# The last layer's slot numbers read by one load, and four result buffers instead of two

## The chip, the cores and the metric

The kernel runs on one core of a Trainium2 chip. The metric is the device time of one execution in microseconds, the median of several runs. The engines are TensorE (PE, matrix products; PEld is its weight load), VectorE (DVE), ScalarE (ACT), GpSimd (POOL) and SyncE (SP), which issues DMAs. Each runs its own instructions in their order, and they wait for each other through semaphores.

## The reference

Four residual layers in a row on `x` of 64 batches x 64 rows x 256, conditioned by 8 numbers per batch. The change touches the last one only, where each batch goes through one of eight experts:

```python
expert = jnp.argmax(opcode_onehot, axis=-1)
up = jnp.einsum('bsd,bhd->bsh', x, W_up[expert]) + b_up[expert][:, None, :]
gate = jnp.einsum('bsd,bhd->bsh', x, W_gate[expert]) + b_gate[expert][:, None, :]
hidden = jax.nn.silu(up) * gate
out = jnp.einsum('bsh,bdh->bsd', hidden, W_down[expert]) + b_down[expert][:, None, :]
x = x + out
```

D is 256 and the hidden width 512. The layers before it are an expert mixture with top 2 of 8 and a shared expert, a layer with a weight matrix mixed per batch, and a low-rank one.

## The kernel before

The last layer takes two batches of the same expert at a time, one on each half of the 128 partitions. With padding there are `G3` = 36 such groups, sorted by expert. Tables in SBUF, computed at the start, hold for each group the two batches to read (`source`), the two rows of the output to write (`dest3`), and the expert's turn (`turn3`). An engine that needs such a number loads it into a register and checks its bounds there.

Each product is made in three passes of high and low parts. One step of group i runs as follows.

- PE: the down product of group i-1 (`down3`, L971, 12 matmuls), the transposes of group i's hidden values (`turn_h`, L959), up and gate of group i+1 (`up_gate3`, L950, 12 matmuls), the transposes of x of group i+2 (`turn_x3`, L935).
- ACT: the high part of h (L1133), silu (L1252), the high part of x (L1133), and the copies of biases into PSUM (L1230), for which it reads `turn3` (`bias_turn`, L1226) twice.
- DVE: the low part of h (`lo`, L1803, 128x512), silu times gate (`hidden3`, L1793), the low part of x (L1803, 128x256), and `finish3` (L1799): the down product of group i-1 plus the residual x goes into a result buffer.
- SP: `put` (L375) reads the two output rows, waits for DVE's result (`y_done`) and stores it with two DMAs (L380). `gather` (L365) reads two batch numbers and loads x of group i+8 into one of `NGATHER` = 8 buffers with two DMAs (L372). Both stand in a loop of three turns with eight groups each; groups 24 to 35 are written out behind it.
- POOL: splits the weights of one expert after the other into high and low parts (L432, L434), three pieces each, into four slots, and waits until the expert that used the slot is done.

The result buffers are two pieces of the tile `FS`, used in turn. DVE may write result i when the stores of result i-2 have landed; each store counts 16 on `out_done`, two per group. SP also loads the biases of the layer's experts (`load_bias3`), the last of them (`bias3_last`) behind the first eight gathers; ACT waits for it ahead of its fifth step.

Of the kernel before, what the change touches and what calls it, by code (L numbers as in the profile page):

```python
# [33 lines left out]
ALU = mybir.AluOpType  # L34
# [4 lines left out]
NB, S, D = 64, 64, 256  # L39
E = 8  # L40
# [15 lines left out]
G3 = (NB + E) // 2  # L56
SLOTS0, SLOTS3 = 2 * NR0, 2 * G3
# [9 lines left out]
NBIAS = 2 * I3 + D  # L67
BSLOTS = NBIAS // D
NGATHER = 8
NONE = NB  # L70
TOP_SCALE = 1.0 / 12
WARM_UP = 12
# [3 lines left out]
def build(nc, x, xT, cond, condT, w0, w1, mask, b1, w2, b2, w3, b3, out):  # L76
# [3 lines left out]
    with ExitStack() as ctx:  # L80
        def sb(name, shape, dt=F32):
            return ctx.enter_context(nc.sbuf_tensor(name, shape, dt))

        def sem(name):
            return ctx.enter_context(nc.semaphore(name))
# [7 lines left out]
        FS = sb("FS", [P, 2560])  # L93
        routing = sb("routing", [P, 1720])
# [7 lines left out]
        source = sb("source", [1, SLOTS], I32)  # L102
        dest3 = sb("dest3", [1, SLOTS3], I32)

        turn0 = sb("turn0", [1, NR0], I32)
        turn3 = sb("turn3", [1, G3], I32)
# [31 lines left out]
        h3h, h3l = RS[:, 512:1024], RS[:, 1024:1536]  # L138
        gathered = [acc[:, BSLOTS * E + k, :] for k in range(NGATHER)]
        act3, hid3 = FS[:, 1024:1536], FS[:, 1536:2048]  # L140
        result = [FS[:, 2048:2304], FS[:, 2304:2560]]


        first_raw = [acc[:, NSH + 4 * i:NSH + 4 * (i + 1), :].rearrange("p a d -> p (a d)") for i in range(6)]
# [29 lines left out]
        up3_ps, gate3_ps, out3_ps = bank[0:2], bank[2:4], bank[6:8]  # L174
# [38 lines left out]
        x3_done, x3_stored = sem("x3_done"), sem("x3_stored")  # L213
        gathered_in = [sem(f"gathered_in{k}") for k in range(NGATHER)]
        t3_done = sem("t3_done")
# [3 lines left out]
        h3h_done, h3l_done = sem("h3h_done"), sem("h3l_done")  # L219
        down3_done = sem("down3_done")  # L220
        y_done = sem("y_done")
        out_done = [sem(f"out_done{p}") for p in range(2)]

        def half_rows(n):
            return slice(S * (n % 2), S * (n % 2) + S)

        block = ctx.enter_context(nc.Block())

        @block.sync
        def _(sp):  # L230
# [119 lines left out]
            def load_bias3(turns, arrived):  # L350
                for t in turns:
                    e = sp.value_load(chosen3[0:1, t:t + 1], min_val=0, max_val=E - 1)
                    sp.dma_start(acc[:, BSLOTS * t:BSLOTS * (t + 1), :].rearrange("p a d -> p (a d)"),
                                 b3[bass.ds(e, 1)].broadcast_to([P, NBIAS])).then_inc(arrived, 16)
# [9 lines left out]

            def gather(i, q, after=None):  # L365

                batches = [sp.value_load(source[0:1, bass.ds(SLOTS0 + 2 * i + j, 1)], min_val=0, max_val=NB - 1)  # L367
                           for j in range(2)]
                if after is not None:
                    sp.wait_ge(x3_stored, 16 * after)  # L370
                for j, b in enumerate(batches):
                    sp.dma_start(gathered[q][S * j:S * (j + 1), :], x3[bass.ds(b, 1)].rearrange("a s d -> (a s) d"))\  # L372
                        .then_inc(gathered_in[q], 16)

            def put(i, p):  # L375
                batches = [sp.value_load(dest3[0:1, bass.ds(2 * i + j, 1)], min_val=0, max_val=NB + SLOTS3 - 1)
                           for j in range(2)]
                sp.wait_ge(y_done, i + 1)
                for j, b in enumerate(batches):
                    sp.dma_start(out[bass.ds(b, 1)].rearrange("a s d -> (a s) d"),  # L380
                                 result[p][S * j:S * (j + 1), :]).then_inc(out_done[p], 16)

            gather(0, 0, after=NU - 1)
            gather(1, 1)
            store_x3(2 * UL - 1, UE + UL - 1)
            gather(2, 2, after=NU)
            for i in range(3, NGATHER):
                gather(i, i)
            sp.wait_ge(x1_done, NU)
            load_bias3((6,), bias3_last)  # L390
            with sp.Fori(0, (G3 - NGATHER) // NGATHER) as ring:
                for q in range(NGATHER):
                    put(NGATHER * ring + q, q % 2)
                    gather(NGATHER * ring + q + NGATHER, q)
            for i in range((G3 - NGATHER) // NGATHER * NGATHER, G3):
                put(i, i % 2)
                if i + NGATHER < G3:
                    gather(i + NGATHER, i % NGATHER)
            for k in range(2):
                sp.wait_ge(out_done[k], 32 * (G3 // 2))  # L400

        @block.gpsimd
        def _(pool):

            def iota(dst, pattern, base, per_partition):
                return pool.iota(dst, pattern=pattern, base=base, channel_multiplier=per_partition,
                                 allow_small_or_imprecise_dtypes=True)

            iota(iota_slot, [[1, SLOTS0]], 0, 0)
            iota(small[:, 0:E], [[1, E]], -E, 0)  # L410
            iota(small[:, 8:9], [[0, 1]], -NONE, 1)
            iota(diag_int, [[-8, 4]], 32, 1)
# [597 lines left out]
        def _(act):  # L1010
# [32 lines left out]
            def stack(n):  # L1043
                k, here = n // 2 % 2, half_rows(n)
                act.wait_ge(masked, n // 2 + 1)
                if n >= 4:
                    act.wait_ge(mixed_in[1], 2 * (n - 4) + 2)
                act.activation(stacked[n % 4][here, :], raw[here, k, :], ACT.Copy).then_inc(stack_hi, 1)
# [174 lines left out]
            ranks_hi(NU - 2)  # L1223

            def bias_turn(i):
                return act.value_load(turn3[0:1, bass.ds(i, 1)], min_val=0, max_val=E - 1)  # L1226

            def bias_in_psum(e, ps, part, slots, done):
                rows_ = acc[:, bass.ds(BSLOTS * e + part, slots), :].rearrange("p a d -> p (a d)")
# [12 lines left out]
            def out_bias(i, p, first=False):  # L1242
                e = bias_turn(i)
                if not first:
                    act.wait_ge(y_done, i - 1)
                bias_in_psum(e, out3_ps[p], 4, 1, out_pre)
# [45 lines left out]
        def _(dve):  # L1292
# [3 lines left out]
            def done(op):  # L1296

                count[0] += 1
                op.then_inc(route_step, 1)
                dve.wait_ge(route_step, count[0])  # L1300

            TT, TS, STT = dve.tensor_tensor, dve.tensor_scalar, dve.scalar_tensor_tensor
# [148 lines left out]
            def route_read_sums():  # L1451

                dve.wait_ge(route_sums, 1)
                for j in range(2):
                    half = slice(S * j, S * (j + 1))
                    dve.tensor_copy(weight0[half, :], turn_ps[0][half, SLOTS + j:SLOTS + SLOTS0:2])
                TS(batch, turn_ps[0][0:1, 0:SLOTS], float(NONE), None, ALU.add).then_inc(route_read, 1)

# [15 lines left out]
            def route_dests():  # L1474
                done(TS(flag, batch, float(NONE), float(NB), ALU.is_ge, ALU.mult))
                done(TT(part, part, flag, ALU.add))
                TS(place[:, :], part, float(NONE), None, ALU.min)

                b3_, f3 = batch[:, SLOTS0:SLOTS], flag[:, SLOTS0:SLOTS]
                done(TS(f3, f3, 1.0 / NB, None, ALU.mult))  # L1480
                done(TT(f3, f3, slot_row[:, :], ALU.mult))
                TT(dest3[:, :], b3_, f3, ALU.add).then_inc(tables_ready, 1)
# [87 lines left out]
            def add(g, p):  # L1570

                batches = [dve.value_load(place[0:1, bass.ds(2 * (g - S0) + j, 1)], min_val=0, max_val=NONE)
                           for j in range(2)]
# [214 lines left out]
            def hidden3(i, p, first=False):  # L1788
                dve.wait_ge(silu_done, i + 1)
                dve.wait_ge(gate3_done, i + 1)  # L1790
                if not first:
                    dve.wait_ge(turnh_done, i)
                TT(hid3, gate3_ps[p][:, :], act3, ALU.mult).then_inc(hid3_done, 1)  # L1793

            def finish3(i, q, first=False):
                dve.wait_ge(down3_done, i + 2)
                if not first:
                    dve.wait_ge(out_done[q % 2], 16 * (i - q % 2))
                TT(result[q % 2], out3_ps[q % 2][:, 0:D], gathered[q], ALU.add).then_inc(y_done, 1)  # L1799

            def lo(i, dst, src, hi, hi_done, done_):
                dve.wait_ge(hi_done, i)
                TT(dst, src, hi.bitcast(F32), ALU.subtract).then_inc(done_, 1)  # L1803

            def step3(i, q, before=True, after=True, first=False, early=False):
                if before:
                    lo(i, h3l, turnh_ps[:, :], h3h, h3h_done, h3l_done)
                hidden3(i, q % 2, first=first)
                if after:
                    lo(i + 2, x3l, turn3_ps[:, 0:D], x3h, x3h_done, x3l_done)  # L1810
                if before:
                    finish3(i - 1, (q - 1) % NGATHER, first=early)
# [1 line left out]
            lo(1, x3l, turn3_ps[:, 0:D], x3h, x3h_done, x3l_done)  # L1814
            finish(NU - 1)
            step3(0, 0, before=False, first=True)
            step3(1, 1, early=True)
            step3(2, 2, early=True)
            step3(3, 3)
            with dve.Fori(0, G3 // NGATHER - 1) as ring:  # L1820
                for k in range(NGATHER):
                    step3(NGATHER * ring + 4 + k, (4 + k) % NGATHER)
            for i in range(G3 - NGATHER, G3):
# [59 lines left out]
```

## Time and profile before

| | us |
|---|---|
| median of 3 runs | 1258.02 (1258.01 to 1258.64) |
| the profiled execution | 1253.87 |
| span of its trace, first to last instruction | 1252.2 |
| TensorE busy in the span | 1216.2 (97%) |
| VectorE busy | 726.4 (58%) |
| ScalarE busy | 475.5 (38%) |
| GpSimd busy | 468.4 (37%) |

The last layer's steps lie between about 1050 us and the end of the span. Matmul rows are pipelined and their ends are modelled. Register instructions and the issuing of DMAs aren't counted as busy, so SP has no busy time in the table; its instructions are seen by line and in the timeline, as SPq.

### The profile page before, as it was taken

To read this page: it belongs to the slowest core of one execution; us is meant where nothing else is said; L and a number is where in the kernel's file an instruction comes from. 1 tells how busy PE (TensorE), PEld (TensorE's weight loads), DVE (VectorE), ACT (ScalarE), POOL (GpSimd) and SP (SyncE) were. 2 spreads that over 40 slices of the span, in tenths; PEclk is the share of its full clock that TensorE was granted. 3 is DMA by queue.
4 is the path that set the end of the run, shared out by engine and by line. 5 is a ranking of instruction groups with operands and counts; after the bars stand their busy time and mean duration, and the time that the engine had idled before them with its cause. 6 is when DMAs were issued, how large, how long until landed. Compare 5 with 4: busy or idle time off the path is not lost.

```text
span 1252.2 us, 27660 instructions
## 1 busy us (share of the span) xinstructions
PE 1216.2 (97%) x7456; PEld 1066.8 (85%) x7457; DVE 726.4 (58%) x1279; ACT 475.5 (38%) x889; POOL 468.4 (37%) x297
## 2 busy tenths in 40 slices
PE   8998999999999999999999999999999998999998
PEld 7898998888888888888888888899999987777887
DVE  6889776556565565565656565555555554333333
ACT  5365522232232322222232232343344334555564
POOL 2177588118062071441718350100000028848500
PEclk9999999999999999999999999999999998999999
DMA  7187862103121021120303120253334354534311
GB/s 219 40 275 269 291 200 80 50 13 100 30 77 52 13 80 50 46 84 13 116 14 112 38 59 17 51 148 93 102 108 113 90 209 134 153 113 118 93 51 40
DMA packets 130997, 123.83 MB, mean 99 GB/s; under 512 B 64512, under 2 KB 114944, under 8 KB 128896
## 3 DMA queue, kind: packets, MB, share of 16 engines
q1 hardware_dynamic: 117264, 73.33, 20.2%
q0 software_dynamic: 13680, 49.81, 13.0%
q8 instruction: 30, 0.49, 0.2%
q14 instruction: 23, 0.19, 0.1%
HBM read 97.42 MB, written 25.69 MB: 98 GB/s over the span
## 4 chain that ended last, share of the span: by engine, by line
PE 81%; SPq 7%; DVE 5%; issue 3%; DMA 1%; POOL 1%; ACT 1%; DVEq 0%; ACTq 0%; POOLq 0%
PE bank L586 15%; PE bank L588 15%; PE bank L587 15%; PE bank L642 10%; PE bank L623 5%; PE bank L641 4%; PE bank L950 3%; PE bank L814 2%; SPq L372 2%; PE bank L693 2%; PE bank L971 2%; SPq L367 2%; SPq L380 2%; PE bank L695 2%; PE bank L694 2%
## 5 line engine op out<-in xcount | busy, mean ns | idle before, releaser
L432 POOL TENSOR_TENSOR W<-raw,one 128x1024 fp32r<-128x1024 f32 x79 | 150.3, 1903 | 585.4 <-PE bank L642 349.6
L1514 DVE TENSOR_TENSOR FS<-bank,FS 128x512 f32<-128x512 f32 x200 | 138.1, 691 | 189.9 <-PE bank L588 162.8
L1029 ACT ACTIVATE FS<-bank 128x512 f32<-128x512 f32 x200 | 119.4, 597 | 321.8 <-PE bank L588 321.6
L586 PE MATMUL bank<-W,RS 128*128 (+1 forms) x576 | 224.8, 390 | 2.0 <-DVE W L1609 1.6
L588 PE MATMUL bank<-W,RS 128*128 (+1 forms) x576 | 224.4, 390 | 0.0
L587 PE MATMUL bank<-W,RS 128*128 (+1 forms) x576 | 224.2, 389 | 0.0
L642 PE MATMUL bank<-W,RS 128*128 x544 | 216.2, 419 | 0.0
L434 POOL TENSOR_TENSOR W<-raw,W 128x1024 fp32r<-128x1024 f32 x79 | 191.9, 2430 | 6.2
L1582 DVE SCALAR_TENSOR_TENSOR acc<-bank,weight,acc 64x256 f32 x272 | 131.6, 484 | 73.3 <-issue 35.7
L1036 ACT ACTIVATE RS<-bank 128x512 fp32r<-128x512 f32 x144 | 86.0, 598 | 172.5 <-PE bank L623 172.5
L586 PE MATMUL bank<-RS,W 128*128 128x256 f32 x448 | 129.1, 288 | 0.0
L587 PEld LDWEIGHTS bank<-W,RS 128*128 128x128 f32 x576 | 108.2, 188 | 23.0
L588 PEld LDWEIGHTS bank<-W,RS 128*128 128x128 f32 x576 | 108.1, 188 | 22.6
L588 PE MATMUL bank<-RS,W 128*128 128x256 f32 x448 | 126.6, 283 | 0.0
L587 PE MATMUL bank<-RS,W 128*128 128x256 f32 x448 | 126.6, 283 | 0.0
L586 PEld LDWEIGHTS bank<-W,RS 128*128 128x128 f32 x576 | 108.4, 188 | 20.1 <-DVE W L1609 2.0
L1518 DVE TENSOR_TENSOR RS<-bank,RS 128x512 fp32r<-128x512 f32 x144 | 99.5, 691 | 29.9 <-ACT RS L1036 28.8
L641 PE MATMUL bank<-W,RS 128*128 x408 | 115.3, 283 | 0.0
L642 PEld LDWEIGHTS bank<-W,RS 128*128 128x128 f32 x544 | 103.1, 189 | 12.8
L950 PE MATMUL bank<-W,RS 128*128 x432 | 108.8, 401 | 0.4 <-issue 0.3
L950 PEld LDWEIGHTS bank<-W,RS 128*128 128x128 f32 x432 | 79.2, 189 | 17.2 <-issue 1.5
L623 PEld LDWEIGHTS bank<-ident,FS 128*128 128x128 f32 x576 | 71.8, 142 | 18.6 <-DVE FS L1514 1.3
(194 smaller groups left out, 2108.9 us busy)
## 6 DMA issues: line engine op xcount, KB each, us to landing
raw<-in_w POOLq DMA_DIRECT2D x87, 512.0 KB, 4.1
mixes<-acc SPq DMA_DIRECT2D x16, 1024.0 KB, 6.0
W<-mixes SPq DMA_DIRECT2D x16, 1024.0 KB, 6.1
FS<-in_xT SPq DMA_DIRECT2D x200, 64.0 KB, 2.5
acc<-in_b SPq DMA_DIRECT2D x8, 640.0 KB, 8.4
acc<-x SPq DMA_DIRECT2D x72, 64.0 KB, 2.1
out_rows<-FS SPq DMA_DIRECT2D x72, 64.0 KB, 2.0
acc<-in_x SPq DMA_DIRECT2D x32, 128.0 KB, 4.0
```

Of the source, the lines that this page charges most:

```text
L432: pool.tensor_tensor(hi, raw[:, k, :], ones_like(PIECE), ALU.mult).then_inc(done, 1)
L434: pool.tensor_tensor(lo, raw[:, k, :], hi.bitcast(F32), ALU.subtract).then_inc(done, 1)
L586: pe.matmul(ps, ah, bh, start=(i == 0), stop=False)
L587: pe.matmul(ps, ah, bl, start=False, stop=False)
L588: mm = pe.matmul(ps, al, bh, start=False, stop=(i == n - 1))
L623: mm = pe.transpose(chunk(turn_ps[h], c), chunk(hid[h], c), ident[:, :])
L641: pe.matmul(ps, chunk(hl[h], c), w2_[:, 0, :], start=False, stop=False)
L642: mm = pe.matmul(both, chunk(hh[h], c), w2_, start=(h == 0 and c == 0), stop=(h == 1 and c == 3))
L950: mm = pe.matmul(ps[:, :], chunk(x, c), w, start=False, stop=(c == 1 and x is x3l), skip_group_check=True)
L1029: act.activation(gl[h], gate_ps[h][:, :], ACT.Gelu_apprx_tanh).then_inc(gelu_done, 1)
L1514: TT(hid[h], up_ps[h][:, :], gl[h], ALU.mult).then_inc(hid_done, 1)
L1582: op = STT(at, out_ps[p][half, D * part_:D * (part_ + 1)], weight0[half, bass.ds(g - S0, 1)], at, ALU.mult, ALU.add)
```

## The change

The two numbers of a `put` or a `gather` are read by one load of two registers, without comparison or assertion; ACT's `bias_turn` also loses its comparison. There are four result buffers, in another part of `FS`, each with a count of its stores. DVE's steps for groups 1 to 11 are written out and its loop covers 12 to 27, since a wait for a count of zero doesn't stand in it.

```diff
+NRESULT = 4
-        result = [FS[:, 2048:2304], FS[:, 2304:2560]]
+        result = [FS[:, D * k:D * (k + 1)] for k in range(NRESULT)]
...
-        out_done = [sem(f"out_done{p}") for p in range(2)]
+        out_done = [sem(f"out_done{p}") for p in range(NRESULT)]
...
+        def table_values(engine, at, top):
+
+            return nc.values_load_multi_w_load_instructions(
+                at, engines=[engine.engine], min_val=0, max_val=top,
+                skip_runtime_bounds_check_because="the routing bounds what the table holds")[1]
...
             def gather(i, q, after=None):
 
-                batches = [sp.value_load(source[0:1, bass.ds(SLOTS0 + 2 * i + j, 1)], min_val=0, max_val=NB - 1)
-                           for j in range(2)]
+                batches = table_values(sp, source[0:1, bass.ds(SLOTS0 + 2 * i, 2)], NB - 1)
...
             def put(i, p):
-                batches = [sp.value_load(dest3[0:1, bass.ds(2 * i + j, 1)], min_val=0, max_val=NB + SLOTS3 - 1)
-                           for j in range(2)]
+                batches = table_values(sp, dest3[0:1, bass.ds(2 * i, 2)], NB + SLOTS3 - 1)
...
-                    put(NGATHER * ring + q, q % 2)
+                    put(NGATHER * ring + q, q % NRESULT)
...
-            for k in range(2):
-                sp.wait_ge(out_done[k], 32 * (G3 // 2))
+            for k in range(NRESULT):
+                sp.wait_ge(out_done[k], 32 * (G3 // NRESULT))
...
             def bias_turn(i):
-                return act.value_load(turn3[0:1, bass.ds(i, 1)], min_val=0, max_val=E - 1)
+                return table_values(act, turn3[0:1, bass.ds(i, 1)], E - 1)[0]
...
                 if not first:
-                    dve.wait_ge(out_done[q % 2], 16 * (i - q % 2))
-                TT(result[q % 2], out3_ps[q % 2][:, 0:D], gathered[q], ALU.add).then_inc(y_done, 1)
+                    dve.wait_ge(out_done[q % NRESULT], 32 // NRESULT * (i - q % NRESULT))
+                TT(result[q % NRESULT], out3_ps[q % 2][:, 0:D], gathered[q], ALU.add).then_inc(y_done, 1)
...
-            step3(1, 1, early=True)
-            step3(2, 2, early=True)
-            step3(3, 3)
-            with dve.Fori(0, G3 // NGATHER - 1) as ring:
+            for i in range(1, NGATHER + 4):
+                step3(i, i % NGATHER, early=i <= NRESULT)
+            with dve.Fori(1, G3 // NGATHER - 1) as ring:
```

On SP, one gather in the loop and the put behind it, before. ISA stands for register instructions (comparison, assertion, address), and a wait belongs to the row that it stands on.

```order
L367 ISA
L367 TENSOR_LOAD source
L367 ISA x3
L367 TENSOR_LOAD source
L367 ISA x2
L372 ISA
L372 DMA acc<-x 64x256
L372 ISA
L372 DMA acc<-x 64x256
```

The same place in the changed kernel, where L230 is the helper that reads the table:

```order
L230 ISA
L230 TENSOR_LOAD source
L378 ISA
L378 DMA acc<-x 64x256
L378 ISA
L378 DMA acc<-x 64x256
L230 ISA
L230 TENSOR_LOAD dest
L383 REGISTER_ALU
L385 ISA [waits y_done]
```

One load and five register instructions are gone ahead of the two DMAs, and the wait for the result stays behind the load.

On DVE, the first steps of the last layer before, from group 2's result on. L1803 is a low part, L1793 silu times gate, L1799 the result.

```order
L1799 TENSOR_TENSOR FS<-bank,acc 128x256 [waits out_done0,down3_done]
L1820 UNCONDITIONAL_BRANCH
L1820 ISA
L1803 TENSOR_TENSOR RS<-bank,RS 128x512 [waits h3h_done]
L1789 REGISTER_ALU
L1793 TENSOR_TENSOR FS<-bank,FS 128x512 [waits turnh_done,gate3_done,silu_done]
L1802 REGISTER_ALU
L1803 TENSOR_TENSOR RS<-bank,RS 128x256 [waits x3h_done]
L1798 ISA [waits down3_done]
L1799 TENSOR_TENSOR FS<-bank,acc 128x256 [waits out_done1]
```

In the changed kernel, from group 3's result on, which is the last without a wait for a store:

```order
L1804 TENSOR_TENSOR FS<-bank,acc 128x256 [waits down3_done]
L1808 TENSOR_TENSOR RS<-bank,RS 128x512 [waits h3h_done]
L1798 TENSOR_TENSOR FS<-bank,FS 128x512 [waits turnh_done,gate3_done,silu_done]
L1808 TENSOR_TENSOR RS<-bank,RS 128x256 [waits x3h_done]
L1804 TENSOR_TENSOR FS<-bank,acc 128x256 [waits out_done0,down3_done]
L1808 TENSOR_TENSOR RS<-bank,RS 128x512 [waits h3h_done]
L1798 TENSOR_TENSOR FS<-bank,FS 128x512 [waits turnh_done,gate3_done,silu_done]
L1808 TENSOR_TENSOR RS<-bank,RS 128x256 [waits x3h_done]
L1804 TENSOR_TENSOR FS<-bank,acc 128x256 [waits out_done1,down3_done]
```

The waits for stores begin at group 4 instead of group 2 and go round over four counts, and there are no register operations between the instructions of the steps written out. PE's and POOL's instructions are the same as before.

## Rows read from the trace of the kernel before

**Rows 1.** Busy time by stretch: stretch, length, then each engine's, PE clock, DMA, GB/s.
```profile
1057.00:1247.00 190.00, 177.82 (x1038) 151.31 (x1037) 71.97 (x139) 106.98 (x204) 88.49 (x54) 0.99 0.34 97
1057.00:1067.00 10.00, 10.00 (x64) 8.84 (x63) 4.28 (x8) 6.57 (x13) 8.49 (x6) 1.00 0.43 123
```

**Rows 2.** Waits from 1057 to 1247: who for whom, us, times, longest.
```profile
DVE FS L1799 <- DMA out_rows<-FS: 82.1, 29, 5.1
...
PE bank L971 <- DVE RS L1803: 9.2, 7, 2.0
```

**Rows 3.** Timeline, undisturbed steps: start, us, engine, line, tiles, [idle before <- releaser].
```profile
1057.20 1.68 PE L971 MATMUL bank<-W,RS 128*128 x12
...
1058.72 0.60 PE L959 MATMUL bank<-ident,FS 128*128 128x128 f32 x4
1058.92 0.42 DVE L1799 TENSOR_TENSOR FS<-bank,acc 128x256 f32<-128x256 f32 x1 [0.57 <-PE bank L971]
1059.08 3.00 PE L950 MATMUL bank<-W,RS 128*128 x12
...
1066.90 1.68 PE L971 MATMUL bank<-W,RS 128*128 x12
```

**Rows 4.** Timeline, a mildly disturbed step.
```profile
1212.83 1.68 PE L971 MATMUL bank<-W,RS 128*128 x12
...
1213.54 1.36 SPq L380 DMA_DIRECT2D out_rows<-FS  x2
...
1216.45 0.42 DVE L1799 TENSOR_TENSOR FS<-bank,acc 128x256 f32<-128x256 f32 x1 [2.48 <-DMA out_rows<-FS]
...
1217.92 1.66 PE L971 MATMUL bank<-W,RS 128*128 x12
```

**Rows 5.** Timeline of SP alone, one turn of its loop.
```profile
1142.09 1.23 SPq L380 DMA_DIRECT2D out_rows<-FS  x2
1144.83 1.22 SPq L372 DMA_DIRECT2D acc<-x  x2
1147.61 1.23 SPq L380 DMA_DIRECT2D out_rows<-FS  x2
```

**Rows 6.** Timeline, the last steps.
```profile
1218.76 1.22 SPq L380 DMA_DIRECT2D out_rows<-FS  x2
...
1238.34 1.68 PE L971 MATMUL bank<-W,RS 128*128 x12
...
1243.04 1.59 PE L971 MATMUL bank<-W,RS 128*128 x12
...
1246.85 1.70 PE L971 MATMUL bank<-W,RS 128*128 x12 [1.78 <-DVE RS L1803]
```

**Rows 7.** Timeline, from the last of the first gathers on.
```profile
1066.85 0.37 SPq L353 DMA_DIRECT2D acc<-in_b  x1
...
1068.90 1.27 SPq L380 DMA_DIRECT2D out_rows<-FS  x2
...
1071.78 0.60 ACT L1133 ACTIVATE RS<-bank 128x512 fp32r<-128x512 f32 x1 [2.87 <-DMA acc<-in_b]
...
1073.52 1.70 PE L971 MATMUL bank<-W,RS 128*128 x12 [1.53 <-DVE RS L1803]
```

**Rows 8.** SP's L376 (reading dest3) and L372's landing: ns min/median/max, first, last start.
```profile
L376 SPq FUSED_REGOPS  x117: 46/152/159, 1067.8 to 1247.3; - x117
L376 SPq TENSOR_LOAD <-dest x72: 262/268/286, 1067.4 to 1247.0; - x72
L376 SPq SEQ_ASSERT  x72: 18/18/18, 1068.0 to 1247.5; - x72
...
DMA to landing us min/median/max: 2.0/2.1/4.0
```

**Rows 9.** Timeline of POOL alone, splits that waited for a slot.
```profile
1126.11 1.88 POOL L432 TENSOR_TENSOR W<-raw,one 128x1024 fp32r<-128x1024 f32 x1 [14.22 <-PE bank L971]
...
1165.24 1.88 POOL L432 TENSOR_TENSOR W<-raw,one 128x1024 fp32r<-128x1024 f32 x1 [3.13 <-PE bank L971]
...
1177.27 2.38 POOL L434 TENSOR_TENSOR W<-raw,W 128x1024 fp32r<-128x1024 f32 x1
```

More of the change, by code:

```diff
@@ L392, in _ @@
                 for q in range(NGATHER):
-                    put(NGATHER * ring + q, q % 2)
+                    put(NGATHER * ring + q, q % NRESULT)
                     gather(NGATHER * ring + q + NGATHER, q)
             for i in range((G3 - NGATHER) // NGATHER * NGATHER, G3):
-                put(i, i % 2)
+                put(i, i % NRESULT)
                 if i + NGATHER < G3:
                     gather(i + NGATHER, i % NGATHER)
-            for k in range(2):
-                sp.wait_ge(out_done[k], 32 * (G3 // 2))
+            for k in range(NRESULT):
+                sp.wait_ge(out_done[k], 32 * (G3 // NRESULT))
         @block.gpsimd
```

## The prediction

> **What bounds the kernel now.** I began with the table of stretches. TensorE (PE) is busy all through the first 10 us after the last layer's first down product, while of the 190 us from 1057 to 1247 it is busy 177.8 [rows 1]. The list of waits for that stretch says who is late: the VectorE (DVE) line L1799, which writes a group's result, waited 29 times, 82.1 us in all, for the DMA that stores an earlier result. TensorE waited for DVE in turn: the list has 9.2 us for line L1803, the low half of h [rows 2].
>
> Then single steps. In undisturbed ones, the down product of a group (L971) starts at 1057.20, the transposes (L959) at 1058.72, up and gate (L950) at 1059.08, and the down product two steps on at 1066.90. A step takes 4.85 us, and TensorE has no gap in it. DVE writes the result at 1058.92, 1.72 us after the down product's start [rows 3]. In a mildly disturbed step the down products start at 1212.83 and 1217.92, 5.09 us apart. SP had issued two stores at 1213.54; DVE waited 2.48 us until one result had left its buffer, at 1216.45, and TensorE's down product, which needs the subtraction behind that result on DVE, came 1.47 us later [rows 4].
>
> The store is late because SyncE (SP) issues it late. With two buffers, result i waits until store i-2 has landed. SP's rows read: two stores from 1142.09 (1.23 us), two gathers from 1144.83 (1.22 us), the next two stores from 1147.61 [rows 5]. That is a turn of 5.52 us, above the 4.85 us of TensorE, in which SP never idles. Of it 1.23 + 1.22 us issue DMAs and 3.07 us, two sections of 1.53 us, read slot numbers. So **SP's instruction stream bounds the last layer**, through the two result buffers.
>
> How much is lost: the first down product starts at 1057.20 [rows 3], the last but two at 1238.34, the last but one at 1243.04, the last at 1246.85 [rows 6]. There are 36, so 35 intervals take 189.65 us. Undisturbed they would take 33 x 4.85, then 4.70 (1238.34 to 1243.04, without transposes of x), then the 3.81 us to the last: 168.6 us. The loss is **21.1 us**. TensorE's idle time of 12.2 us is less than that, since its ends are modelled and rows behind a wait are drawn longer; starts are the safer measure. One interval has a second cause: the down product of 1073.52 also came after ScalarE (ACT) had waited for the last bias row until 1071.78. SP had issued that row only at 1066.85, behind its gathers [rows 7].
>
> **The change, part by part.** *One load, no comparison.* On SP a slot number costs a load (268 ns), a comparison (152 ns) and an assertion (18 ns) [rows 8]. A section of two has these twice, and in the loop an address per number (about 50 ns, the short form of the same operation, 46 ns at least). The change removes one load, two comparisons, two assertions and one address: 0.268 + 0.304 + 0.036 + 0.05 = 0.66 us. It removes six instructions, each with some 0.04 us before it: the two numbers of a section take 2 x (0.268 + 0.152 + 0.018) + 0.10 = 0.98 us of the 1.53, and the other 0.55 us are the descriptor's registers and such pauses between the section's instructions. So 0.24 us more go, 0.90 in all, and a section is left with 0.62 us. The new turn is 1.23 + 1.22 + 2 x 0.62 = **3.69 us**.
>
> A load of two registers is in no row. Below it can't cost less than a load of one, 0.27 us. Above, the nearest row is two loads, 0.54 us, which gives a turn of 4.23 us. I take 0.27 to 0.54; both are under 4.85, so the result doesn't depend on it. The point from which it does is (4.85 - 3.69) / 2 = 0.58 us above 0.27: a load of 0.85 us.
>
> The Trainium skill ("Runtime: NRT & Kernel Launch", section "Instruction fetch mechanics") gives about 200 ns per register for such loads and says that bulk doesn't help; by it a load of two takes an estimated 0.4 us and the turn 3.95 us. The same page's launch section has a TENSOR_LOAD of about 1.3 us, of several registers from HBM. That price would undo the edit: the turn would be 5.75 us. The row of 268 ns is of a table in SBUF and speaks for the smaller one.
>
> *Where the stall goes.* Five gathers (groups 3 to 7) and the first put lie between the arrival of the last x3 and SP's first store at 1068.90 [rows 7]. At about 0.84 us less each (0.90 in the put) the bias row is issued at 1066.85 - 5 x 0.84 = 1062.7 and, at its present 4.9 us to landing, is there at 1067.6. ScalarE needs it when the fourth transposes end, at 1069.0 (1057.20 + 2 x 4.85 + 1.52 + 0.60). This stall goes, with 1.4 us to spare. The first store starts at 1068.90 - 5.1 = 1063.8. From there stores follow at 1063.8 + 3.69 i until they meet the results at 1059.5 + 4.85 i, near group 4; then SP waits for DVE and not DVE for SP.
>
> *Four buffers.* Result 4 is the first that needs a buffer back: store 0 has it free 2.9 us behind its issue (1213.54 to 1216.45 [rows 4]), at 1066.7, and the result comes at 1078.3 (1057.20 + 4 x 4.85 + 1.72), 11.6 us later. With SP in time, two buffers would do as well: 2.9 us and the 0.6 us from result to issue (0.42 for the result, some 0.2 to pass it on) are 3.5 us, against 9.7 us of two steps. So these parts share one gain. In the order, the DVE waits now alternate over four counts, and the eight steps of groups 4 to 11 are written out; that removes register operations and adds none per step. The two further waits at SP's end cost some 0.04 us each. Behind SP's wait for a result stand the gathers of group i+8; they are issued about 2.5 us behind the start of result i, land 2.1 us later [rows 8], and are wanted six steps on.
>
> *ScalarE.* It reads two numbers a step and loses the comparison and the assertion, 0.17 us each time by the rows of SP [rows 8]. In undisturbed steps TensorE has no gap [rows 3], so I count nothing.
>
> *What is late next.* GpSimd's weights come nearer. Its splits wait for a slot until a down product ends: 14.22 us until 1126.11, 3.13 us until 1165.24 [rows 9]. Those are the ends of groups 12 and 19, so the slots come free at 1117.1 and 1151.0. The last expert's three pieces took from 1165.24 to 1179.65 (the last row, 1177.27 + 2.38); started at 1151 they end at 1165.4, and the ones before it also keep their pace. Counting the groups by expert as the table orders them (7, 6, 3, 4, 3, 2, 4, 4) the last starts at group 29, whose up product begins at 1057.2 + 27 x 4.85 + 1.9 = 1190. There are 24 us in hand.
>
> *Sum.* Every step at 4.85 us: 1246.85 - 21.1 = 1225.8 for the last down product, and the end behind it as now. Against the profiled execution that is 1253.87 - 21.1 = 1232.8 us. That execution lies 4.15 us under the median of the runs, 1258.02 us; the profile doesn't say why. I subtract the same 21.1 us from the median: **1237 us**.
>
> **The rivals.** *(a) Only the buffers help*: SP's turn stays near its 5.6 us, because the removed comparisons are paid elsewhere or the load of two is slow (1.2 us and more). Store 27 now goes at 1218.76 [rows 6]; with two buffers it bounds group 29, with four group 31. Then the last down product starts at 1218.76 + 2.91 + 1.47 + 4.85 + 4.70 + 3.81 = 1236.5, 10.4 us earlier than now: 1247.6 us. For it speaks that a load of two has no row; against it that the comparison has one. A related case gives nearly the same time: without the profiler SP runs faster than in it, and so less was lost than 21.1 us; half of it would be 10.5 us.
>
> *(b) The step doesn't hold at 4.85 us.* Steps of 5.09 us, where DVE's wait is only 2.48 us [rows 4], may hide another limit that comes up once SP is in time; the undisturbed ones [rows 3] speak against it. If all 33 were 5.09 us long, 7.9 us of the gain would go: 1245 us.
>
> *(c) Slower than before.* A load of two registers takes 1.5 us: the turn is 6.15 us, the first store at 1070.8, store 27 at 1070.8 + 27 x 6.15 = 1236.9, and the last down product, by the terms of (a), 17.7 us later at 1254.6, 7.8 us after now's: 1265.8 us. It decides from about 1.4 us a load, five times the row of a single one.
>
> *(d) No change*, within 0.2% (2.5 us, about what a measurement of this kernel can tell): the lost time returns at another wait, as weights or a slower clock. Granted clock 0.99 over the stretch [rows 1] leaves little room for the latter.
>
> **How the numbers follow.** The forecast has 0.76 (1234 to 1240 us by itself: 21.1 us with 3 either way, for steps that stay disturbed and for the pace without profiler); (a) 0.09, (b) 0.08, (c) 0.03, (d) 0.04. The range must leave out at most 0.2, and reaches to (b) and nearly to (a): 1233 to 1246 us. Faster takes the forecast, (a) and (b): 0.93; the same 0.04; slower 0.03.
>
> **What would show it.** The wait of DVE's result line for the store goes from 82.1 us to nearly nothing and the line waits for TensorE instead; SP's queue appears among the waiting, for DVE's result, once per group from about group 4; SP's two stores stand 4.85 us apart; the last layer's down products are 4.85 us apart throughout; a load of two registers takes between 0.27 and 0.54 us; ScalarE no longer waits for the bias row. A turn of SP above 4.85 us in the first groups, or steps of 5.1 us without any wait for a store, would prove me wrong.

## The result and the profile after

The changed kernel takes 1235.63 us (median of 4 runs, 1233.67 to 1237.44), the kernel before 1258.33 us in the same series. The ratio is 0.9819, 95% interval 0.9803 to 0.9834: 22.7 us less. The profiled execution of after took 1234.94 us, 18.9 us less than that of before, whose 1253.87 us lay under its median.

The lines of the changed kernel have moved: L976 is the down product (L971 before), L964 the transposes of h, L955 up and gate, L1804 DVE's result, L1138 ScalarE's high parts, L385 SP's stores, L378 its gathers, L360 its bias row, L230 the reading of slot numbers.

First the table of stretches, for the last layer's steps and their first 10 us; the columns are those of [rows 1].

```profile
1057.00:1226.00 169.00, 168.58 (x1043) 149.16 (x1041) 73.85 (x138) 106.31 (x205) 90.71 (x55) 1.00 0.38 113
1057.00:1067.00 10.00, 10.00 (x63) 8.85 (x62) 4.28 (x8) 6.31 (x13) 8.46 (x6) 1.00 0.55 173
```

TensorE is now busy in 168.6 of 169 us, where 12.2 us of 190 were idle. The list of waits from 1057 to 1226, and below it SP's own from 1040 on:

```profile
DVE FS L1804 <- PE bank L976: 20.9, 35, 0.7
...
POOL W L437 <- PE bank L976: 4.9, 1, 4.9
...
ACT RS L1138 <- DMA acc<-in_b: 1.2, 1, 1.2
```

```profile
SPq L385 <- DVE FS L1804: 33.0, 23, 3.0
```

The row of [rows 2], DVE's 82.1 us for stores, has no successor. DVE's result now waits only for the down product, 0.6 us a time, and SP waits for DVE, 23 times. The direction of the wait has turned round, though not from the start. These rows are the result and the two stores of group 0, and then those of group 12:

```profile
1060.13 0.42 DVE L1804 TENSOR_TENSOR FS<-bank,acc 128x256 f32<-128x256 f32 x1 [0.57 <-PE bank L976]
...
1067.97 1.28 SPq L385 DMA_DIRECT2D out_rows<-FS  x2
...
1119.01 0.42 DVE L1804 TENSOR_TENSOR FS<-bank,acc 128x256 f32<-128x256 f32 x1 [0.67 <-PE bank L976]
...
1119.60 1.22 SPq L385 DMA_DIRECT2D out_rows<-FS  x2
```

The first store is issued 7.4 us behind its result. SP catches up by group 12, and from there on each store follows its result by 0.16 us. TensorE has no wait for the low half of h in this stretch.

The timeline, first and last steps:

```profile
1058.41 1.68 PE L976 MATMUL bank<-W,RS 128*128 x12
...
1063.33 1.68 PE L976 MATMUL bank<-W,RS 128*128 x12
...
1068.18 1.68 PE L976 MATMUL bank<-W,RS 128*128 x12
```

```profile
1219.02 1.68 PE L976 MATMUL bank<-W,RS 128*128 x12
...
1223.73 1.59 PE L976 MATMUL bank<-W,RS 128*128 x12
...
1227.54 1.69 PE L976 MATMUL bank<-W,RS 128*128 x12 [1.78 <-DVE RS L1808]
```

From the first to the last down product are 169.13 us, against 189.65 before: 20.5 us less. The stage began 1.2 us later in this execution (1058.41 for 1057.20), and its end behind the last down product is 0.4 us longer; taken off the 20.5 us, these two leave the 18.9 us between the profiles.

Where it came from stands in SP's timeline, two turns of its loop in the first groups, when it never waits, and in the view of the line that reads the numbers:

```profile
1076.31 1.22 SPq L385 DMA_DIRECT2D out_rows<-FS  x2
1078.34 1.21 SPq L378 DMA_DIRECT2D acc<-x  x2
1080.41 1.22 SPq L385 DMA_DIRECT2D out_rows<-FS  x2
1082.43 1.21 SPq L378 DMA_DIRECT2D acc<-x  x2
1084.50 1.22 SPq L385 DMA_DIRECT2D out_rows<-FS  x2
```

```profile
L230 SPq FUSED_REGOPS  x45: 51/69/85, 1069.3 to 1174.1; - x45
L230 SPq TENSOR_LOAD <-source x36: 463/474/581, 1040.1 to 1193.5; - x36
L230 SPq TENSOR_LOAD <-dest x36: 465/476/494, 1067.2 to 1227.1; - x36
```

A turn takes 4.10 us instead of 5.52 [rows 5]. The DMA issues are as long as before; the two sections between them shrank from 1.53 to about 0.83 us. A load of two registers takes 474 ns, one of one register took 268 [rows 8]. The operations of 152 ns and the assertions are gone; what is left under FUSED_REGOPS are the short ones, of 69 ns in the median.

### The profile page after: what moved, and what is told of

It reads as the page before. It is cut to its first block, busy times and chain, and to the rows that moved or that the text cites. A ratio compares the mean times of both kernels' runs of the same rounds, so it can differ in the third digit from the quotient of the medians.

```text
span 1233.3 us, 27095 instructions
## 1 busy us (share of the span) xinstructions
PE 1206.0 (98%) x7456; PEld 1064.0 (86%) x7457; DVE 727.3 (59%) x1279; ACT 474.4 (38%) x889; POOL 468.6 (38%) x297
## 3 DMA queue, kind: packets, MB, share of 16 engines
q1 hardware_dynamic: 117264, 73.33, 20.5%
## 4 chain that ended last, share of the span: by engine, by line
PE 92%; DVE 4%; issue 1%; POOL 1%; DMA 1%; ACT 1%; SPq 0%; DVEq 0%; ACTq 0%; POOLq 0%
PE bank L591 15%; PE bank L593 15%; PE bank L592 15%; PE bank L647 10%; PE bank L955 8%; PE bank L628 5%; PE bank L976 4%; PE bank L646 4%; PE bank L819 2%; PE bank L698 2%; PE bank L700 2%; PE bank L699 2%; PE bank L964 1%; PE bank L649 1%; PE bank L858 1%
## 5 line engine op out<-in xcount | busy, mean ns | idle before, releaser
L955 PE MATMUL bank<-W,RS 128*128 x432 | 108.0, 399 | 0.5 <-issue 0.4
L955 PEld LDWEIGHTS bank<-W,RS 128*128 128x128 f32 x432 | 78.5, 188 | 15.9 <-issue 1.0
```

Source lines behind the costliest of these rows:

```text
L955: mm = pe.matmul(ps[:, :], chunk(x, c), w, start=False, stop=(c == 1 and x is x3l), skip_group_check=True)
```

## The experiments

Times are medians, each with its ratio to runs of the kernel before on the same chip. Kernels of one batch ran side by side.

### First batch: which half of the change brought the gain

**The changed kernel again**, as a measure.

> The changed kernel once more, unaltered, as the measure for the other runs on this chip. Theory (SP's turn of 5.5 us was the bound, now 4.10 us): the down products stand 4.85 us apart, ratio to before 0.982 as first measured, between 0.980 and 0.984.

1237.29 us, ratio 0.9832 (0.9818 to 0.9846). The change holds; the size is 21 us here.

**Only the reading**, with two buffers.

```diff
-NRESULT = 4
+NRESULT = 2
```

> The changed kernel with two result buffers instead of four; the reading of slot numbers stays changed. Theory A (the gain is all SP's turn, the buffers add nothing once SP is in time): the time of the changed kernel within 1 us, but for the start of the layer, where SP begins late with its stores (group 0 at 1067.97) and DVE may wait one or two times: 0 to 2 us more. Rival (both parts are needed; with two buffers DVE goes on waiting for stores): half of the gain or less, 1245 us or more.

1237.30 us, ratio 0.9836 (0.9823 to 0.985): the same as the whole change. Two rows of its lists of waits, DVE's and SP's:

```profile
DVE FS L1804 <- DMA out_rows<-FS: 2.9, 2, 1.8
```

```profile
SPq L385 <- DVE FS L1804: 34.8, 26, 3.0
```

With two buffers DVE waits for a store twice, 2.9 us in all, in the first groups; of the step that holds them TensorE loses 0.07 us (4.92 for 4.85). Theory A holds: once SP is in time, the further buffers add nothing.

**Only the buffers.**

```diff
-                batches = table_values(sp, source[0:1, bass.ds(SLOTS0 + 2 * i, 2)], NB - 1)
+                batches = [sp.value_load(source[0:1, bass.ds(SLOTS0 + 2 * i + j, 1)], min_val=0, max_val=NB - 1)
+                           for j in range(2)]
```

and likewise in `put` and in ScalarE's `bias_turn`.

> The changed kernel with the old way of reading numbers on SP and ScalarE (two loads, comparison, assertion); four result buffers stay. Theory A: SP's turn is 5.5 us again and bounds the stage, and the two more buffers are worth two of the late steps once, 10.4 us under before: about 1247 us. Rival B (buffers take all the waits away): about 1236 us. Rival C (the buffers are worth nothing): about 1258 us.

1250.85 us, ratio 0.9949 (0.9934 to 0.9963): 7.2 us under before, nearest to A, but 3 us short of its 10.4. DVE still waits (first row), and the trace says where the 3 us are. These are the rows of its last down product and result, and of SP's stores (L387 here).

```profile
DVE FS L1806 <- DMA out_rows<-FS: 48.6, 18, 4.3
```

```profile
1237.49 1.70 PE L978 MATMUL bank<-W,RS 128*128 x12 [1.78 <-DVE RS L1810]
1239.23 0.42 DVE L1806 TENSOR_TENSOR FS<-bank,acc 128x256 f32<-128x256 f32 x1 [2.16 <-PE bank L978]
```

```profile
L387 SPq MOVE out_rows<-FS x72: 29/29/36, 1069.2 to 1243.8; - x72
```

The last down product starts at 1237.49, 9.4 us earlier than before (1246.85 [rows 6]); the sum of rival (a), taken from this run's store 27 at 1219.13, gives 1219.13 + 17.7 = 1236.8. But the last result is ready at 1239.65 and the last store is issued only at 1243.8. SP's list of waits holds none for a result: it is behind to the very end, a further 3 us or so that rival (a) left out by taking the end "as now". In the kernel before, two buffers held DVE so near to SP that SP, with no more gathers to issue from group 28 on, caught up by group 32, and the last store followed its result at once.

**The bias row earlier.**

```diff
             gather(2, 2, after=NU)
+            sp.wait_ge(x1_done, NU)
+            load_bias3((6,), bias3_last)
             for i in range(3, NGATHER):
                 gather(i, i)
-            sp.wait_ge(x1_done, NU)
-            load_bias3((6,), bias3_last)
```

> The changed kernel with the last bias row issued by SP behind the third gather instead of behind the eighth. Theory: the one step that is still long (5.33 us, ScalarE waits 1.24 us for the bias row) becomes 4.85 us, 0.5 us in all, at the edge of what can be measured, and the wait for the row disappears from the list of waits. Rival: the gathers that are now behind it come late for the transposes of x, and 1 us or more is lost.

1235.11 us, ratio 0.9824 (0.9807 to 0.984), beside 0.9832 for the changed kernel. In its trace the down products stand at 1059.25, 1064.10, 1068.94, 1073.79 and 1078.64, all 4.85 us apart, and the wait for the bias row is gone from the list. By its time it can't be told from the changed kernel.

### Second batch: is it SP's turn against the step, and what are buffers good for

**Two single loads without comparison**, two buffers.

```diff
-                batches = table_values(sp, dest3[0:1, bass.ds(2 * i, 2)], NB + SLOTS3 - 1)
+                batches = [table_values(sp, dest3[0:1, bass.ds(2 * i + j, 1)], NB + SLOTS3 - 1)[0]
+                           for j in range(2)]
```

and the same in `gather`.

> Two result buffers, and each slot number on SP read by a load of its own, without comparison and assertion. Theory (what counts is only whether SP's turn is under TensorE's step of 4.85 us): two single loads with their addresses take 0.80 us where the load of two takes 0.60, so the turn goes from 4.10 to about 4.5 us, still under the step, and the time is that of the kernel with two buffers and one load, 1236 to 1239 us. Rival (joining the two loads is what brought the gain): about 1245 us or more.

1236.74 us, ratio 0.9833 (0.9809 to 0.9857). The turn is 4.5 us in its trace (stores at 1148.01 and 1152.48), under the step, and the whole gain is there. Joining the loads wasn't needed.

**One load, comparisons kept**, two buffers.

```diff
+        def checked_values(engine, at, top):
+            return nc.values_load_multi_w_load_instructions(
+                at, engines=[engine.engine], min_val=0, max_val=top)[1]
...
-                batches = table_values(sp, dest3[0:1, bass.ds(2 * i, 2)], NB + SLOTS3 - 1)
+                batches = checked_values(sp, dest3[0:1, bass.ds(2 * i, 2)], NB + SLOTS3 - 1)
```

and the same in `gather`.

> Two result buffers and one load of two slot numbers, but with the comparison and the assertion for each number on SP. Theory: about 0.5 us more in each section, a turn of 5.1 us, above the step; store 27 at about 1208.7, the last down product 27.4 us behind it, at 1236 instead of 1228: about 8 us more than without comparison, 1245 us. Rival (the comparisons lie beside the DMAs and cost nothing): 1237 us.

1247.73 us, ratio 0.9922 (0.9903 to 0.9941): 11 us more than the kernel above, where 8 were expected, and 9.7 us under before. Its line of reading from 1075 to 1160 shows what is left, and DVE waits for stores again:

```profile
L235 SPq FUSED_REGOPS  x96: 51/152/165, 1075.1 to 1159.6; - x96
L235 SPq SEQ_ASSERT  x66: 18/18/26, 1075.3 to 1159.8; - x66
L235 SPq TENSOR_LOAD <-dest x17: 470/474/476, 1074.6 to 1158.9; - x17
```

```profile
DVE FS L1808 <- DMA out_rows<-FS: 54.5, 23, 3.9
...
ACT RS L1142 <- DMA acc<-in_b: 2.6, 1, 2.6
```

Its turn is 5.18 us (stores at 1081.01 and 1086.19). The expectation put the store of group 27 at about 1208.7 and the last down product 27.4 us behind it. They came here:

```profile
1212.10 1.22 SPq L389 DMA_DIRECT2D out_rows<-FS  x2
...
1239.65 2.65 PE L980 MATMUL bank<-W,RS 128*128 x12 [1.78 <-DVE RS L1812]
```

The distance is 27.5 us, as the theory had it. The store is 3.4 us late, because SP's first one went out at 1070.59, 2.6 us later than assumed, and its turns average 5.24 us. In the kernel above the last down product starts at 1229.83, 9.8 us earlier. Another 0.95 us is in the last down product itself: it took 2.65 us, at a granted clock of 0.57 in the 2.8 us from 1239.6, where the kernel above took 1.70 us at 1.00. Without comparisons the turn is under TensorE's step, with one load or with two. Joining the loads alone takes part of the surplus away, and with it 9.7 of before's some 21 us.

**A slow SP with four and with two buffers.** Both take the changed kernel and put two unused checked loads into each gather from group 8 on; the second has two buffers.

```diff
+                for _ in range(spare):
+                    sp.value_load(source[0:1, 0:1], min_val=0, max_val=NB - 1)
...
-                    gather(NGATHER * ring + q + NGATHER, q)
+                    gather(NGATHER * ring + q + NGATHER, q, spare=2)
```

> The changed kernel with four buffers and two further, unused loads with comparison (0.56 us each) in every gather from group 8 on: SP's turn 4.10 + 1.12 = 5.2 us, above the step of 4.85. Theory (four buffers forgive a late SP by two steps more): store 27 at 1067.97 + 27 x 5.2 = 1208.9, bound for the last down product 17.7 us later at 1226.6, before the 1227.5 that TensorE sets: no change, 1236 to 1239 us. Rival (a turn over the step costs at once what it is over it): 27 x 0.37 = 10 us more.

> The same two further loads per gather, with two buffers. Theory: the last down product comes 27.4 us behind store 27, at 1236.3 instead of 1227.5: about 8.8 us more than with four buffers at the same turn, 1246 us. Rival (buffers make no difference even when SP is late): the time of the four-buffer kernel with the same loads.

Four buffers: 1237.88 us, ratio 0.9845 (0.9827 to 0.9863). Two buffers: 1246.70 us, ratio 0.9918 (0.9899 to 0.9937). The difference is 8.8 us, as expected, at a turn of 5.24 us in both (the commonest turn; the mean is 5.3). DVE's waits for stores, four buffers and then two:

```profile
DVE FS L1806 <- DMA out_rows<-FS: 20.1, 10, 2.7
```

```profile
DVE FS L1806 <- DMA out_rows<-FS: 65.8, 30, 4.2
```

So a turn above the step isn't lost at once. With four buffers SP's store lies 5.8 us behind its result at group 0 and 17.9 us at group 24, about 0.5 us more with each group, and from there DVE waits each time up to group 32. From then to the end TensorE's steps lose 1.4 us together. For a turn of 5.52 us, as the kernel with only the buffers shows, four don't suffice: there DVE waits from group 15 on and TensorE's steps are long from group 17 on. The last down products came at 1230.29 (four buffers) and 1238.63 (two), where 1227.5 and 1236.3 were expected. Both are some 2.5 us late, and 0.7 us of the difference is a slower clock in the last down product of the second (2.41 us at a granted 0.64, for 1.69 us). So that it came out at just 8.8 us is partly luck.

### Third batch: the small parts

**The changed kernel again**, as a measure.

> The changed kernel unaltered, as the measure for the two beside it: 0.983 of before.

1236.56 us, ratio 0.9832 (0.9819 to 0.9845).

**ScalarE's comparison back.**

```diff
-                return table_values(act, turn3[0:1, bass.ds(i, 1)], E - 1)[0]
+                return act.value_load(turn3[0:1, bass.ds(i, 1)], min_val=0, max_val=E - 1)
```

> The changed kernel with ScalarE's number read as before, with comparison and assertion. Theory: ScalarE has room in a step, so the time is that of the changed kernel within 1 us. Rival (ScalarE's register work delays the copies that TensorE waits for): 2 us or more slower.

1234.99 us, ratio 0.9816 (0.9803 to 0.983). It is not slower: 1.6 us under its neighbour, with overlapping intervals. That part of the change does nothing that can be measured.

**The bias row earlier**, the same kernel a second time.

> The kernel with the bias row issued earlier, once more beside the changed one. Theory: 0.5 us less by the trace, which is at or below what the runs can tell; their intervals overlap, and the trace has no wait of ScalarE for the bias row.

1238.22 us, ratio 0.9839 (0.9826 to 0.9853), this time 1.7 us above its neighbour. Of the two pairs one points each way. The wait is gone in both traces, and from the first to the last down product they have 168.43 and 168.67 us, where three traces of the changed kernel have 169.13, 169.83 and 170.15. So within the stage half a microsecond to one and a half goes; as a time of the kernel it isn't measured.

## Why the prediction was right, point by point

- *The bound.* SP's instruction stream, acting through the result buffers, was what held the last layer. Shown from both sides: comparisons back at one load, slower by 11 us; unused loads added to SP, 8.8 us slower with two buffers than with four; SP shortened by the reading alone, the whole gain. The sum of rival (a), by which the last down product comes 17.7 us behind the store of group 27 with four buffers, and two steps later, 27.4 us, with two, fits every changed kernel whose SP is late to within a microsecond: 27.5 us with one load and comparisons, 27.8 and 18.0 with the unused loads, 18.4 with only the buffers.
- *The loss of 21.1 us.* The down products of after take 169.13 us for a computed 168.6; the gain within the stage is 20.5 us. Timed: 22.7, 20.7 and 20.9 us in three series. The sum from the profile, 1232.8 us, is 2.1 us short of the 1234.94: the stage began 1.2 us later, one step stayed long by 0.5 us, and the end took 0.4 us more.
- *The clock* (rival d). The trace of before holds one stretch in this stage in which TensorE was granted half its clock (the lower level, 1.2 GHz). It came shortly behind 1.99 us in which TensorE waited for DVE. The columns of the first row are those of [rows 1]:

```profile
1138.00:1141.00 3.00, 3.00 (x14) 2.81 (x14) 0.04 (x1) 0.98 (x2) 2.92 (x2) 0.50 0.84 224
```

```profile
1136.95 2.48 PE L971 MATMUL bank<-W,RS 128*128 x12 [1.99 <-DVE RS L1803]
...
1140.96 0.42 DVE L1799 TENSOR_TENSOR FS<-bank,acc 128x256 f32<-128x256 f32 x1 [3.50 <-DMA out_rows<-FS]
```

  The result of that step waited 3.50 us for a store even so, and SP's turns around it stay at 5.51 and 5.52 us. The slower clock was hidden behind SP, and in after the stage has 1.00 throughout.
- *The load of two.* It was left between 0.27 and 0.54 us and is 0.474, so the turn is 4.10 us and not the 3.69 that was the lower bound, within the 4.23 of the upper. The result didn't hang on it, as said. The Trainium skill ("Runtime: NRT & Kernel Launch", section "Instruction fetch mechanics") has about 200 ns per register, in bulk too. Here it is 237 ns a register in a load of two and 268 in a load of one, so the rule comes near; the second register adds 206 ns. The 1.3 us of that page's launch table (section "The launch sequence") occurs in none of these loads from a table in SBUF.
- *When SP catches up.* The prediction had the first store at 1063.8 and SP waiting from near group 4, once per group. The store went out at 1067.97, SP met the results only at group 12, and its list has 23 waits. The prediction had two things too fast: the gathers ahead of the first store (see the bias row) and the turn of 3.69 us. Neither cost time at the result buffers, since store 0 had landed at 1072.6, 7.5 us before DVE began result 4.
- *Two buffers would do as well.* Shown: 1237.30 beside 1237.29 us.
- *The step of 4.85 us holds* (rival b). But for the two last, shorter ones, all steps of the profile but one are within 0.1 us of it; the 5.09 us of [rows 4] were the mild form of the same wait.
- *GpSimd.* It waited for a slot once, 4.9 us, instead of 19.6 us in three; TensorE never waited for weights.
- *The bias row.* This step failed in part. The prediction said that the wait goes "with 1.4 us to spare". It stayed, 1.2 us of ScalarE's time and one step of 5.33 us (1073.09 to 1078.42). The bias row went out at 1066.63, not at 1062.7, and two terms were wrong. The first is the start: SP's first gather behind the last x3 was assumed at its old 1052.31 and came at 1054.47, since x3 was stored 1.07 us later in this execution and its gather was issued 3.6 us behind the store instead of 2.5. The down products began 1.2 us later too, so this alone would have used up 1.0 of the 1.4 us to spare. The second and larger one is the pace, 0.84 us saved in each gather, which was worked out with the lower bound for the load: from the first gather to the bias row SP took 12.16 us instead of 10.3. These rows are the first part of that path and its end:

```profile
1050.88 0.38 SPq L336 DMA_DIRECT2D x<-raw  x1
...
1054.47 1.14 SPq L378 DMA_DIRECT2D acc<-x  x2
```

```profile
1066.63 0.37 SPq L360 DMA_DIRECT2D acc<-in_b  x1
...
1071.32 0.60 ACT L1138 ACTIVATE RS<-bank 128x512 fp32r<-128x512 f32 x1 [1.24 <-DMA acc<-in_b]
```

Its price is 0.5 us, within the range. SP's gathers of groups 2 and 7 start at 1054.47 and 1064.33, 9.86 us apart instead of 12.65, and not 8.45 as five times 0.84 us less would give. Of these 1.4 us, 1.0 is the longer load, 0.2 us a gather. One DMA issue of group 6's gather took 1.30 us in place of 0.47, the first row here; the same stretch of before had slower spots of its own, of 0.45 us together. Whether ScalarE waits goes with that one issue. It took 1.77 us in a second trace of the changed kernel, whose row is the second, and 1.68 us in a third, and in all three ScalarE waited. In the kernels with only the reading, the third row, and with ScalarE's comparison back, which have the same order on SP, that issue took 0.47 us, and ScalarE didn't wait. Why it is sometimes long wasn't tried.

```profile
1062.34 1.30 SPq L378 DMA_DIRECT2D acc<-x  x1
```

```profile
1063.91 1.77 SPq L378 DMA_DIRECT2D acc<-x  x1
```

```profile
1061.98 0.47 SPq L378 DMA_DIRECT2D acc<-x  x1
```

*Rival (a)* was measured as "only the buffers", and its 10.4 us were 3 us too many, since a late SP also ends late. The related case in it, that SP is faster without the profiler, is tested by no run here.

## What to carry to other kernels

When a wait names the landing of a DMA, look at when the DMA was issued, and if its queue never idles, count that engine's turn, register instructions included, against the step of the bound engine. Above the step its size counts: here 0.7 us a group too much cost 21 us, and 0.3 us too much 11. Under the step nothing more is to be had: 0.35 us under it did as well as 0.75, however it was reached. In these runs two more buffers forgave a late engine once, by at most their number times the step, and didn't make it faster. They are worth having where the two rates are close, and they hide a backlog that may come back at the end, as the 3 us did here.

## What the runs showed that was not expected

A load of two registers from one instruction took 474 ns against 2 x 268 = 536 ns for two, so joining them saves 0.06 us for the load itself; a comparison with its assertion costs 0.17 us and the pauses around them. Of the 1.4 us taken from SP's turn about 1.0 went with the comparisons and assertions (5.52 to 4.5 us with two single loads), the rest with joining the loads.

The start of the last layer moves by some microseconds from execution to execution: the last x3 was stored at 1049.81 in the profile of before and at 1050.88, 1052.56 and 1054.12 in three profiles of the same changed kernel. ScalarE waited for the bias row 1.2, 1.9 and 1.8 us in these three. A late start isn't enough for that: the kernel with ScalarE's comparison back stored x3 at 1052.06 and had no such wait. The cause of the movement wasn't tried.
